# A gated state-space layer with a routed expert on one core: softplus by one table function, another share of the B products, C products in single groups

## The reference

```python
# layer 1: state-space mixing; z = layernorm(x), hidden = ctx (4, 1024, 512)
x_ = silu(causal_conv4(hidden @ in_proj_w.T) + conv_b)        # 1024 channels d
dt_low, B, C = split(x_proj_w @ x_, [32, 16, 16])
dt = softplus(dt_proj_w @ dt_low + dt_proj_b)
for t in range(1024):                                         # 16 states n per channel
    state = state * exp(dt[t] * A) + (dt[t] * x_[t]) * B[t]   # A = -exp(A_log)
    y[t] = sum_n(state * C[t])
x = x + tanh(g_xattn) * ((y + D * x_) * silu(z))
# layer 2: expert choice routing over 4096 tokens
S = softmax(layernorm(x) @ router_w + router_b)               # 16 experts
G, idx = top_k(S.T, 256)                                      # each expert takes 256 tokens
x = x + tanh(g_ffn) * scatter_add(G * (layernorm(x)[idx] @ expert_w + expert_b))
```

## Time and profile before

| | |
|---|---|
| Median of three runs | 2504.0 us |
| Profiled execution | 2504.36 us, its span 2502.6 us, mean granted clock 0.803 |
| Busy | TensorE 1764.2, VectorE 2150.8, ScalarE 1324.0, GpSimd 1975.7 us |
| Scan stage (first to last scan of VectorE) | 68 to 2047 us |
| Tail | 2047 to 2119 us |
| Search | 2119 to 2191 us |
| Expert products | 2191 us to the end |

### The profile page before, as it was taken

The page is one execution under the profiler, slowest core; times in us unless marked ns, Lnnn a source line. Parts: engine busy times, 40 slices in busy tenths (PEclk is TensorE's granted clock), DMA queues, the critical chain, the costliest instruction groups (busy, mean ns, idle before and its releaser), DMA issues.

```text
span 2502.6 us, 28548 instructions
## 1 busy us (share of the span) xinstructions
PE 1764.2 (70%) x8120; PEld 1358.1 (54%) x8120; DVE 2150.8 (86%) x2438; ACT 1324.0 (53%) x2269; POOL 1975.7 (79%) x778
## 2 busy tenths in 40 slices
PE   6466756766667667666766676666666764999998
PEld 2245444555545554545555555454555554778887
DVE  7999999999999999999999999999999974663343
ACT  3547565756575657565756575657565742111111
POOL 0689999999999999999999999999999984122221
PEclk8677877877787778777877787778777875999999
DMA  9401150134014311331143114211421136054441
GB/s 357 191 18 43 33 226 14 56 109 162 31 60 143 125 31 59 146 123 31 60 145 122 35 56 154 114 52 40 179 105 40 48 124 215 9 206 139 150 151 67
DMA packets 74841, 260.76 MB, mean 104 GB/s; under 512 B 8993, under 2 KB 11681, under 8 KB 63553
## 3 DMA queue, kind: packets, MB, share of 16 engines
q1 hardware_dynamic: 74688, 259.01, 29.0%
HBM read 208.05 MB, written 50.92 MB: 103 GB/s over the span
## 4 chain that ended last, share of the span: by engine, by line
DVE 27%; issue 25%; POOL 21%; PE 20%; ACT 5%; DVEq 1%; DMA 1%; POOLq 0%; ACTq 0%; SPq 0%
DVE states L1038 14%; POOL states L1347 14%; PE pDec L754 10%; DVE states L1025 5%; POOL states L1335 4%; PE pU L754 3%; DVE u L1010 2%; PE pY L628 2%; POOL sp L1316 1%; ACT pDec L848 1%; PE pA L596 1%; PE pT L663 1%; DVE sp L1015 1%; DVE szT L1062 1%; DVE stats L1092 1%
## 5 line engine op out<-in xcount | busy, mean ns | idle before, releaser
L1347 POOL TENSOR_TENSOR states<-states,cbc 128x2048 f32<-128x2048 f32 x256 | 1158.5, 4532 | 95.0 <-ACT carry L831 44.8
L848 ACT ACTIVATE pDec<-dt,an 128x512 f32<-128x512 f32 x1024 | 696.3, 688 | 693.2 <-DVE states L1038 691.8
L628 PE MATMUL pY<-con,states 128*128 128x128 f32 x4096 | 725.0, 352 | 408.2 <-POOL states L1347 407.8
L628 PEld LDWEIGHTS pY<-con,states 128*128 128x128 f32 x4096 | 663.4, 188 | 462.2 <-POOL states L1347 457.4
L1038 DVE TENSOR_TENSOR_SCAN states<-pDec,carry,states 128x512 f32<-128x512 f32 x512 | 625.8, 1264 | 11.7 <-ACT pDec L848 11.0
L1038 DVE TENSOR_TENSOR_SCAN states<-pDec,states 128x512 f32<-128x512 f32 x512 | 594.9, 1204 | 15.3 <-ACT pDec L848 14.6
L1335 POOL TENSOR_TENSOR states<-dtu,bbc 128x1024 f32<-128x1024 f32 x193 | 457.0, 2368 | 10.6 <-PE pY L628 6.7
L1025 DVE TENSOR_TENSOR states<-pU,bbc 128x1024 f32<-128x1024 f32 x320 | 385.7, 1205 | 6.6 <-ACT pU L826 3.6
L596 PE MATMUL pA<-ctx_sb,win 128*128 128x512 f32 x536 | 260.4, 631 | 22.4 <-ACT szT L860 8.6
L1293 DVE TENSOR_TENSOR u<-u,sp 128x1024 f32<-128x1024 f32 x32 | 67.9, 2122 | 168.6 <-ACT u L984 168.5
L984 ACT COPY u<-pDec 128x512 f32<-128x512 f32 x48 | 26.6, 589 | 318.1 <-PE pDec L754 147.2
(11 more groups left out here) (169 smaller groups left out, 2377.4 us busy)
## 6 DMA issues: line engine op xcount, KB each, us to landing
bbc<-bc_scratch SPq DMA_DIRECT2D x35, 1024.0 KB, 5.5
cbc<-bc_scratch SPq DMA_DIRECT2D x34, 1024.0 KB, 6.8
win<-in_winT SPq DMA_DIRECT2D x71, 256.0 KB, 2.7
sz<-in_x SPq DMA_DIRECT2D x16, 1024.0 KB, 4.9
xt<-in_x SPq DMA_DIRECT2D x8, 2048.0 KB, 8.0
x_scratch<-xt SPq DMA_DIRECT2D x8, 2048.0 KB, 8.2
xt<-x_scratch SPq DMA_DIRECT2D x32, 512.0 KB, 4.4
out<-u SPq DMA_DIRECT2D x32, 512.0 KB, 3.0
```

Of the source, the lines that this page charges most:

```text
L628: mm = pe.matmul(pY[:, eT(t)], states[g % NST][:, i, eT(t)], ident, start=False, stop=(q == QG - 1 and i == QN - 1 and t == TT - 1), is_tr ...
L848: nc.scalar.activation(pDec[turn][:], dt[e % 2][:], ACT.Exp, scale=an[:, k:k + 1]).then_inc(s_dec, 1)
L1347: nc.gpsimd.tensor_tensor(st, st, cbc[:, QW * q:QW * (q + 1), :], ALU.mult).then_inc(s_hc, 1)
```

## The change

- `softplus` becomes one ScalarE instruction, Softplus, straight from bank pD into dt. `log1p`, `log1p_rest` and `step_size` go. Softplus is in another activation table than Exp, so a table load stands before it and another behind it. The chain starts ten slots ahead of its channel and not twelve. dt lives in a tensor `steps`.
- `POOL_GROUPS`: GpSimd makes the B product of groups 1, 3, 5, 7 of even channels and of 1, 4, 7 of odd ones; before, 1, 4, 7 of all.
- `times_c` handles one group, 128x1024, and stands one slot behind its scans; `sum_states` follows two slots later.
- The logits go to bank pD, ScalarE copies them (`logits_out`), and VectorE adds the bias once per half row in `softmax_in`.
- Some slots of the input projection, of Silu and of the gate are moved.
- All hardware loops are written out.

```diff
-IN_SLOT = [-83] + [GQ * j - 85 for j in range(1, E)]
+IN_SLOT = [-77, -73] + [GQ * j - 85 for j in range(2, E)]
-HALO_SLOT, SILU_SLOT = [-25], [-23]
-XP_SLOT, LOW_SLOT = [-21, -21, -20, -20], [-18]
-DTP_SLOT = [GQ * e - 12 for e in range(E)]
-SP_SLOT = [GQ * e - 10 for e in range(E)]
-LN_SLOT = [GQ * e - 9 for e in range(E)]
-REST_SLOT = [GQ * e - 8 for e in range(E)]
-DT_SLOT = [GQ * e - 6 for e in range(E)]
+HALO_SLOT, SILU_SLOT = [-24], [-21]
+XP_SLOT, LOW_SLOT = [-19, -19, -18, -18], [-16]
+DTP_SLOT = [GQ * e - 10 for e in range(E)]
+SP_SLOT = [GQ * e - 8 for e in range(E)]
 DTU_SLOT = [GQ * e - 6 for e in range(E)]
-POOL_GROUPS = [g for g in range(NG) if g % QG in (1, 4, 7)]
+POOL_GROUPS = [g for g in range(NG) if g % QG in ((1, 3, 5, 7), (1, 4, 7))[g // QG % 2]]
-CM_SLOT = [2 * i + 2 for i in range(NP)]
-SUM_SLOT = [g - g % 2 + 4 for g in range(NG)]
+CM_SLOT = [g + 1 for g in range(NG)]
+SUM_SLOT = [g + 3 for g in range(NG)]
-SZT_SLOT = [GQ * e + 9 for e in range(E)]
+SZT_SLOT = [GQ * e + 9 for e in range(5)] + [43, 49, 65]
-XFP_SLOT = [90 + 8 * f for f in range(2 * TT)]
-XFT_SLOT = [s + 2 for s in XFP_SLOT]
-LG_SLOT = [100 + 16 * t for t in range(TT)]
+XFP_SLOT = [91 + 8 * f for f in range(2 * TT)]
+XFT_SLOT = [s + 1 for s in XFP_SLOT]
+LG_SLOT = [105 + 16 * t for t in range(TT)]
...
             def softplus(b, o, e):
-                k = n(b, o, 2 * E, 2 * e)
                 wait(act, s_dtm, n(b, o, E, e + 1))
-                wait(act, s_pc, n(b, o, 2 * E, 2 * e))
-                bias = dtb[:, e:e + 1]
-                nc.scalar.activation(sp4[:, 0, :], pD[:], ACT.Abs, bias=bias).then_inc(s_spa, 1)
-                nc.scalar.activation(sp4[:, 3, :], pD[:], ACT.Relu, bias=bias)
-                act.wait_ge(s_spa, k + 1)
-                nc.scalar.activation(sp4[:, 0, :], sp4[:, 0, :], ACT.Exp, scale=-1.0).then_inc(s_spa, 1)
+                wait(act, s_dt, n(b, o, E, e - 1))
+                wait(act, s_dec, n(b, o, NU, NS * (e - 1)))
+                nc.scalar.activation(dt[e % 2], pD[:], ACT.Softplus, bias=dtb[:, e:e + 1]).then_inc(s_sp, 1)
...
-                    if silus or gates:
-                        nc.scalar.preload_act_table_set(EXP_LN)
+                    if steps_due or silus or gates:
+                        nc.scalar.preload_act_table_set(EXP)
...
+            def logits_out(b, o, t):
+                wait(act, s_lgm, n(b, o, TT, t + 1))
+                if t == 0:
+                    wait(act, s_sm, n(b, o, 6, 0))
+                nc.scalar.copy(lg[:, t, :], pD[:, 0:NX]).then_inc(s_lga, 1)
...
-            def logits_in(b, o, t):
-                wait(dve, s_lgm, n(b, o, TT, t + 1))
-                nc.vector.tensor_tensor(lg[:, t, :], pT[:, 0:NX], rb[:], ALU.add).then_inc(s_lga, 1)
...
             def softmax_in(b, o):
                 dve.wait_ge(s_lga, n(b, o, TT, TT))
+                nc.vector.tensor_tensor(lg[:], lg[:], rb[:].rearrange("p (a s) -> p a s", a=1).broadcast_to([P, TT, NX]),
+                                        ALU.add).then_inc(s_sm, 1)
...
-                if o % HB == 0:
-                    wait(pool, s_carry, b * NG + 2 * (i + 1))
-                else:
-                    wait(pool, s_scan, n(b, o, NU, QW * (i + 1)))
-                st = pairs[i % (NST // 2)][:]
-                nc.gpsimd.tensor_tensor(st, st, cbc[:, QW * q:QW * (q + 1), :], ALU.mult).then_inc(s_hc, 1)
+                if o % HB == 0:
+                    wait(pool, s_carry, b * NG + (g + 1))
+                else:
+                    wait(pool, s_scan, n(b, o, NU, QN * (g + 1)))
+                st = states[g % NST][:]
+                nc.gpsimd.tensor_tensor(st, st, cbc[:, QN * q:QN * (q + 1), :], ALU.mult).then_inc(s_hc, 1)
...
-            with dve.Fori(1, B) as b:
+            for b in range(1, B):
```

More of the change, by code:

```diff
@@ L170, in mamba_moe @@
         xpr = sb("xpr", [2 * R, T])
-        pairs = [sb(f"states{i}", [P, 2 * QN, T]) for i in range(2)]
+        states = [sb(f"states{i}", [P, QN, T]) for i in range(4)]
         carry = sb("carry", [P, E, NS])
@@ L201, in mamba_moe @@
             cbc = scan_sb("cbc", [P, NS, T])
-            pairs += [scan_sb(f"states{i}", [P, 2 * QN, T]) for i in range(2, NST // 2)]
-            states = [t[:, QN * i:QN * (i + 1), :] for t in pairs for i in range(2)]
+            states += [scan_sb(f"states{i}", [P, QN, T]) for i in range(4, NST)]
         whi = sb("whi", [P, E, D], F32R)
@@ L313, in tiles_of @@
             return [t[:, 2 * i:2 * i + 2, :].rearrange("p s t -> p (s t)") for i in range(t.shape[1] // 2)]
-        stage = [x for t in (bbc, *pairs, cbc, sz) for x in tiles_of(t)]
+        stage = [x for t in (bbc, *states, cbc, sz) for x in tiles_of(t)]
         stage += [xt[:, t, :] for t in range(TT)] + [xr[0][:], xr[1][:]]
@@ L336, in mamba_moe @@
         pC = [[pDec[0], pDec[1]], [pDec[2], pU]]
-        srt, junk, gtm, eqm, cum, sele, ones = (pairs[i // 4][:, i % 4, :] for i in range(7))
+        srt, junk, gtm, eqm, cum, sele, ones = (states[i // 2][:, i % 2, :] for i in range(7))
         @block.sync
@@ L568, in step @@
                     load_lt(c + 1, t - 1, k + (TT - 1))
-            with sp.Fori(1, NC - 1) as c:
+            for c in range(1, NC - 1):
                 for t in range(TT):
@@ L654, in turn_xf, with logits @@
                 mm.then_inc(s_xfp, 1)
-            def logits(b, o, t, last=False):
+            def logits(b, o, t, steps_read, last=False):
                 wait(pe, s_xfT, n(b, o, 2 * TT, 2 * t + 2))
-                wait(pe, s_lga, n(b, o, TT, t))
+                wait(pe, s_sp, steps_read)
                 for f in range(2):
@@ L728, in _ @@
                 half(0, h, h)
-            with pe.Fori(1, B) as b:
+            for b in range(1, B):
                 for h in range(HB):
@@ L776, in _ @@
                     product_rows(k % TT, k, kk)
-            with pe.Fori(2, NC) as c:
+            for c in range(2, NC):
                 for t in range(TT):
@@ L901, in late @@
                         xfT_out(b, o - k, f, k == least)
+                for t, k in at(LGA_SLOT, g, began):
+                    if k >= least:
+                        logits_out(b, o - k, t)
                 for t, k in at(XF_SLOT, g, began):
@@ L956, in _ @@
                 half(0, h, h)
-            with act.Fori(1, B) as b:
+            for b in range(1, B):
                 for h in range(HB):
@@ L991, in _ @@
                 high_tile((t + 2) % TT, t + 2)
-            with act.Fori(1, NC - 1) as c:
+            for c in range(1, NC - 1):
                 for t in range(TT):
@@ L1261, in _ @@
             for p in range(4):
-                with dve.Fori(parts[p], parts[p + 1]) as i:
+                for i in range(parts[p], parts[p + 1]):
                     search(i)
@@ L1302, in _ @@
             cut_tile(TT - 1, 2 * TT - 1, 1)
-            with dve.Fori(1, NC - 1) as c:
+            for c in range(1, NC - 1):
                 for t in range(TT):
@@ L1404, in _ @@
                 half(0, h, h)
-            with pool.Fori(1, B) as b:
+            for b in range(1, B):
                 for h in range(HB):
@@ L1427, in _ @@
                 low_tile(t, t)
-            with pool.Fori(1, NC) as c:
+            for c in range(1, NC):
                 for t in range(TT):
```

136 lines of the change are left out of this document (53 added, 83 removed).

## The result

The changed kernel takes 2627.14 us (median of four runs, 2616.49 to 2636.79) against 2503.88 for the kernel before beside it: ratio 1.0488, 95% interval [1.0445, 1.0531]. It is slower by 123 us where 112 us less were forecast. The profiled execution took 2616.49 us, the shortest of the four, its span is 2614.7, 112 us more than before. I read it in the order of the prediction.

A forecast was written before the change was run, and what follows sets the result against it. VectorE was taken to bound the scan stage, with GpSimd almost level. From 2504.4 us, 104 came off the stage (1979 to 1875) and 8 off the tail: 2392 us, range 2345 to 2468, its own range alone 2365 to 2420.

The forecast's parts named there:

- The rest: Everything outside the scan stage's main terms: TensorE's transposes at no cost, tail 8 us less, written-out loops 0, expert stage unchanged.
- rival D: Decay queue on ScalarE: every Softplus block costs VectorE 2.2 us, 141 in place of 13; 2520 us, chance 0.06.
- VectorE's work: VectorE's busy time in the scan stage, forecast to fall from 1895.85 to 1809 us.
- Port relief, -10: Scan stage: shorter C products on GpSimd shorten the waits of small VectorE operations by 10 us, bounds 0 and 20.
- Softplus block, 13 us: Load, Softplus, load on ScalarE, 3.25 us per channel, delays VectorE's decays 0.2 us each, 13 us in sum.
- The drain: ScalarE table switches: the skill's page adds 1380 ns to each load's 1283; the forecast did not count it.
- GpSimd: GpSimd in the scan stage: 1832 us busy, a floor of 1856 with waits, level with VectorE's 1862.
- rival C: GpSimd becomes the bound and keeps waiting 126 us beside its work, stage 1958; 2475 us, chance 0.10.
- The larger share, -38.6: Scan stage: 32 of the 320 B products leave VectorE for GpSimd, 38.6 us less VectorE work.
- 13 us of coupling: Scan stage: VectorE and GpSimd, two level engines, run slower than the slower one's pace; 13 us, bounds 0 and 60.
- Written-out loops, 0: Straight code in place of hardware loops changes nothing; 0 us, bounds -8 and +8.
- Tail, -8: After the scan stage, VectorE waits less for router logits; 8 us off, bounds -20 and +8.

The follow-up runs named there:

- both_slots: The changed kernel with transposes, their copies and the sums all back in the slots from before the change; 2476.6 us, ratio 0.9886.
- port_free: both_slots with the `cur` copy moved from VectorE to ScalarE and three softmax steps (bias add, subtraction, product) to GpSimd; 2420.6 us.
- port_free_relu: port_free with Relu in place of Softplus and no table loads around it, so another step size is computed; 2385.2 us.
- before_ports: The kernel before with loops written out, the `cur` copy moved to ScalarE, and the softmax subtraction and product to GpSimd; 2462.1 us.
- turn_first: The changed kernel with only the transposes one slot earlier and copied out two slots behind, as before the change; 2493.0 us, ratio 0.9955.
- no_loads: both_slots with Relu in place of Softplus and no table loads around it, so another step size is computed; 2482.2 us.
- port_free4: port_free with four decay banks; 2370.6 us, ratio 0.9459.

## Why the prediction was wrong

The sign was wrong by one step, and it is in the part headed **The rest**: "TensorE transposes the same tiles, now after every group; it has 660 us of room in the stage", costed at nothing. Room is a share of busy time; what counted was what stands ahead of four short transposes on an in-order queue, and what that waits for. Moved back, 134 to 151 us return. The order on ScalarE and GpSimd, where the terms of the sum lay, was worked through, and that on TensorE, where the tables of the sums and the transposes had changed, was not. The signs named as wrong did appear (a wait for decays of 264 us, over 100), but I had tied them to the Softplus block, rival D, and that is not what made them: the block cost 0.55 to 0.6 us and not 2.2. So the time ended beyond D (2520) by a mechanism that was none of the rivals.

With the order put right the forecast of 2392 would still have missed by 85 us, too low. Of the 84 in the stage of both_slots 39 are work, 31 of them the small groups (67.1 us for 36), and 45 are idle time: the wait for decays is 87.2 us where 25.6 and 13 were counted.

The other steps, one by one:

- **VectorE's work.** Forecast 1809 us in the stage, measured 1824. Its removed terms came as priced (B products at 1.204, L1015 and L1103 gone, the wait of 43.3 gone); the small groups account for 3.7 of the 15, the rest is not traced.
- **Port relief, -10.** The four small groups took 39.9 us in the changed kernel, forecast 36, but there GpSimd idled 282 us. With the slots put right they stood 42.1, 16.5, 7.2 and 1.3 us, 67.1 in all, and moving them gave 56. The step assumed that a small step waits for the end of one product. Some do; the bias add stood for two or five in a row, and for those a shorter product is no relief.
- **Softplus block, 13 us.** Its parts are as priced (1283 and 688 ns; forecast 1.283 and 0.679), its cost was 35 (port_free against port_free_relu), between the forecast and the upper bound of 70. The argument that 4.8 us of cover meet 4.8 us of absence was about right, but "about even" cost 0.55 us and not 0.2. The drain that the prediction weighed does not show here either: 87 loads at L923 have 1.6 us of idle before them.
- **GpSimd.** 512 products at 2.361 us (forecast 2.368), busy 1814 in the stage (forecast 1832). Right within 18 us. The sum of rival C mixes two end points, though: its 1985 us run to the end of GpSimd's work and its 1859 and 1979 do not. To one end point it is 1826 + 120 = 1946 us for the stage, 33 less, so C should have stood at 2463 and not at 2475.
- **The larger share, -38.6.** Worth 11 us in the one kernel where it was tested, that with four banks; the saved time mostly became a wait for decays. There the prediction's "two level engines" had come true with GpSimd ahead, and the 13 us of coupling were too small: VectorE idled 80 us of the stage and GpSimd 44.
- **Written-out loops, 0.** They gave 8 us, at the edge of the bound.
- **Tail, -8.** It is 3 us shorter.

With both hidden causes taken away on both sides, and loops written out on both, the change is worth 41.5 us (before_ports 2462.1 to port_free 2420.6), not 112. That gain is real; the order that the new slot tables made cost more than three times as much. Of the kernels that compute the reference's result, only those with a fourth bank and without the small steps on VectorE came under the forecast's 2392.

## What to carry to other kernels

When a change shifts slot tables, print the order on every engine that anything waits for, the idle ones above all, and ask of each short instruction what long wait stands right ahead of it; an engine with a third of its time free can still be the one that is late. Before trusting a saving on an engine, look for rings: here VectorE's own add released the sum that held the transposes that held its decays. And look at the mean duration of tiny instructions: 1.5 us for 64 numbers a partition, where a free one takes 0.22, is a wait that no list of waits shows, and it can grow when something else is sped up.

## What the runs showed of the hardware

- Some small VectorE operations on SBUF stand while GpSimd runs its products: `tensor_tensor` over 128x64 with two operands in SBUF, and `tensor_scalar` over 128x16. Means over the stage went from 0.22 us free to 5.9 (turn_first) and 7.0 (both_slots) for the bias add, and to 7.6 for `cur` (no_loads). The longest took 10.4 us, over five products, and 13.4 us, over six products and a `dtu`. Others, the eight `cur` of both_slots among them, ended 0.03 us behind the product that ran, with GpSimd's next instruction following at once, so a pause of GpSimd is not needed in every case. Such time counts as busy.
- Not every operation on SBUF does this. In port_free4 49 of the 64 `bn_stats` over 128x512 (L1081) ran wholly inside one GpSimd product and took 0.67 to 0.68 us, and so did 6 of the 8 maxima over 128x64 (0.21 to 0.22). `tensor_scalar` over 128x1 kept 0.14 to 0.15. The large operations that share VectorE's queue (scans with pDec, B products with pU) have one operand in PSUM and took 1.204 to 1.209 us, 1.264 to 1.268 with a carry, in every kernel with three decay banks.
- A Softplus between two table loads took 1.28 + 0.69 + 1.28 us, with no idle time at the loads beyond 0.02 us each.
- Straight code in place of hardware loops, with the same instructions, was 8 us faster of 2504.
